# Expert layers of a decoder: blocks' results added to per-token sums in DRAM inside the loop, in place of a store by slot and a gather at the end

## What is computed

```python
logits = h @ gate_w.T                                  # h: [1024, 256]
scores = jax.nn.softmax(logits.astype(jnp.float32), axis=-1)
topk_w, topk_idx = jax.lax.top_k(scores, K)
cw = jnp.zeros((T, E), jnp.float32)
cw = cw.at[jnp.arange(T)[:, None], topk_idx].add(topk_w)
for e in range(E):
    g = h @ w_gate[e].T
    u = h @ w_up[e].T
    out = jax.nn.silu(g) * u @ w_down[e].T
    y = y + cw[:, e:e + 1].astype(x.dtype) * out
x = x + y
```

## Time and profile before

| | |
|---|---|
| three runs, us | 2011.71, 2017.87, 2011.18 (median 2011.71) |
| profiled execution, us | 2005.86 |
| its span, first to last instruction, us | 2004.0 |
| mean granted PE clock | 0.809 of full speed |
| PE busy | 1119.7 us (56%) |
| DVE busy | 1142.7 us (57%) |
| ACT busy | 473.7 us (24%) |
| POOL busy | 595.1 us (30%) |
| queue of SP's DMAs | 144.47 MB, 24.3% of 16 DMA engines |
| queue of POOL's DMAs | 31.26 MB, 5.9% |
| queue of ACT's DMAs | 19.93 MB, 3.1% |

### The profile page before, as it was taken

One profiled execution on the slowest core, in us unless ns is written; L12 is line 12 of the kernel. 1 busy time (PEld: TensorE's weight loads), 2 busy tenths in 40 slices (PEclk: granted clock), 3 DMA queues, 4 the chain that ended last, 5 costly groups with the idle time before them and its releaser, 6 DMA issues. The chain is left out here.

```text
span 2004.0 us, 21287 instructions
## 1 busy us (share of the span) xinstructions
PE 1119.7 (56%) x5620; PEld 707.5 (35%) x5620; DVE 1142.7 (57%) x1850; ACT 473.7 (24%) x881; POOL 595.1 (30%) x588
## 2 busy tenths in 40 slices
PE   5325536886054862552596704697566378537760
PEld 2202124664023640211354503575333034335540
DVE  5659974333354545998876694311357477463333
ACT  2143302221011444330211101332122266212220
POOL 0026614333620111661200081134302122043325
PEclk9659968998577886997798856899878599868985
DMA  6024335886307302331000011206500500357763
GB/s 203 2 85 147 104 106 167 261 263 188 94 8 147 45 2 87 130 121 63 0 0 1 0 16 27 85 1 181 174 8 2 170 21 3 121 160 213 220 191 102
DMA packets 146192, 196.51 MB, mean 98 GB/s; under 512 B 35056, under 2 KB 109954, under 8 KB 145484
## 3 DMA queue, kind: packets, MB, share of 16 engines
q1 hardware_dynamic: 109996, 144.47, 24.3%
q0 software_dynamic: 12608, 31.26, 5.9%
q10 hardware_dynamic: 23520, 19.93, 3.1%
HBM read 153.55 MB, written 41.75 MB: 97 GB/s over the span
## 5 line engine op out<-in xcount | busy, mean ns | idle before, releaser
L163 PE MATMUL psum<-w_ident,h 128*128 128x128 f32 x144 | 32.9, 423 | 188.3 <-DVE h L144 188.3
L453 PE MATMUL psum<-l0s_conv_out,w_ident 128*128 128x512 f32 x128 | 65.0, 632 | 83.4 <-DVE l0s_conv_out L550 83.4
L453 PE MATMUL psum<-l1s_conv_out,w_ident 128*128 128x512 f32 x128 | 65.6, 638 | 81.3 <-DVE l1s_conv_out L550 81.3
L1481 DVE TENSOR_REDUCE l3x_neg<-psum 128x2 f32<-128x512 f32 x128 | 80.9, 684 | 49.7 <-PE psum L1353 49.7
L163 PEld LDWEIGHTS psum<-w_ident,h 128*128 128x128 f32 x144 | 29.2, 224 | 191.7 <-DVE h L144 179.5
L175 ACT ACTIVATE hT<-psum 128x512 f32<-128x512 f32 x40 | 21.7, 595 | 310.4 <-PE psum L163 268.7
L933 PE MATMUL psum<-l0f_w_in,l0f_xT 128*128 128x352 f32 x224 | 79.1, 476 | 22.2 <-issue 12.4
L1456 ACT ACTIVATE l3x_work<-psum 128x512 f32<-128x512 f32 x128 | 72.5, 599 | 65.0 <-PE psum L1375 64.7
L152 POOL TENSOR_SCALAR rstd<-moments 128x8 f32<-128x8 f32 x12 | 2.9, 240 | 281.6 <-DVE moments L140 281.6
L933 PE MATMUL psum<-l3f_w_in,l3f_xT 128*128 128x192 f32 x256 | 64.5, 381 | 39.2 <-DMA l3f_w_in<-in_l3f_w_in 18.6
L419 POOL TENSOR_TENSOR l1s_xpad<-l1s_du,l1s_bc 128x1024 f32<-128x1024 f32 x32 | 75.2, 2352 | 32.5 <-DVE psum L546 32.4
(11 more groups left out here) (604 smaller groups left out, 3211.3 us busy)
## 6 DMA issues: line engine op xcount, KB each, us to landing
l0f_w_in<-in_l0f_w_in SPq DMA_DIRECT2D x56, 352.0 KB
l0s_bc<-l0s_scratch SPq DMA_DIRECT2D x16, 1024.0 KB, 5.1
l1s_bc<-l1s_scratch SPq DMA_DIRECT2D x16, 1024.0 KB, 5.2
l3f_w_in<-in_l3f_w_in SPq DMA_DIRECT2D x64, 192.0 KB
l0f_w_down<-in_l0f_w_down SPq DMA_DIRECT2D x56, 176.0 KB
l2f_w_in<-in_l2f_w_in SPq DMA_DIRECT2D x24, 352.0 KB
l3f_y_rows<-h SPq DMA_DIRECT2D x16, 512.0 KB, 6.8
l3f_y_rows<-l3f_y ACTq DMA_DIRECT2D x64, 128.0 KB
```

The source lines that it names most:

```text
L163: ins = nc.tensor.transpose(m.psum[:, at:at + P], m.h[:, t, k * P:(k + 1) * P], m.ident[:])
L453: ins = nc.tensor.matmul(m.pair(2 + c)[:, cols], lhsT=m.ident[:], rhs=rhs[:, cols], start=start, stop=stop, skip_group_check=True)
L1481: ins = nc.vector.tensor_reduce(self.neg[k % 2][:, :, hl], bank[:, 0:self.keys].rearrange("p (q k) -> p q k", q=self.maxima), AX_X, ALU.ma ...
```

## The change

The kernel keeps two arrays of per-token sums in DRAM, `sums[0]` and `sums[1]`, of 1024 rows and 128 more that take what unused slots give. SP sets them before the loop: zeros, or the residual in `sums[0]` where there is no shared expert. `h_rows` gets E more columns with the token's combine weights, so that a gather brings the weights along (`x` is [128, 256 + E]); where weights are divided by their sum, that is done earlier. In the gate multiplication DVE takes the weight as the scalar, in a column that it finds from the block's expert (a `value_load` per block). The `y` that leaves PSUM is thus weighted. POOL adds it to one of the two sums, even blocks to one and odd ones to the other, by an indirect transfer with `compute_op=ALU.add`, six blocks behind its gathers; an add waits until the add before it on the same side has landed. A gather now waits for `gate_done`, since `x` is needed until then. DVE's copy of `y` waits for `y_free`, which POOL raises with its adds. After the loop SP waits for all adds and loads both sums in four quarters into `m.h` and `m.hT`, and DVE adds them. The stores of `y`, the fills of `y_rows`, `slot_index`, `weight`, `back` and the final gathers are gone. The token table holds the token's number plus one, so that an unused slot is known by its zero.

```diff
-    x = ring("x", [P, D], GROUP)
+    x = ring("x", [P, D + E], GROUP)
...
-    h_rows = nc.dram_tensor(tag + "h_rows", (T, D), F32).ap()
-    y_rows = nc.dram_tensor(tag + "y_rows", (BLOCKS * P, D), F32).ap()
+    h_rows = nc.dram_tensor(tag + "h_rows", (T, D + E), F32).ap()
+    sums = [nc.dram_tensor(tag + f"sum{i}", (T + P, D), F32).ap() for i in range(2)]
+    landed = [m.h[:], m.hT[:].rearrange("p k (t d) -> p (k t) d", d=D)]
+    QUARTERS = 4
...
+    ADD_LAG = GROUP + 2
...
# SP
-            with sp.Fori(FEWEST, GROUPS) as i:
-                sp.dma_start(y_groups[bass.ds(i, 1)].rearrange("o b p d -> p (o b) d"),
-                             m.h[:, 0:GROUP, :]).then_inc(filled, 16)
+            sp.wait_ge(zeroed, 1)
+            for i in range(2):
+                start = m.resid[:] if i == 0 and not shared else zeros[:].unsqueeze(1).to_broadcast([P, TILES, D])
+                sp.dma_start(of_tiles(sums[i][0:T, :]), start).then_inc(sums_set, 16)
+                sp.dma_start(sums[i][T:, :], zeros[:]).then_inc(sums_set, 16)
+            sp.wait_ge(combined, 1)
+            sp.dma_start(of_tiles(h_rows[:, D:]), combine[:]).then_inc(h_stored, 16)
...
             by_steps(sp, groups, step, 0)
+            for i in range(2):
+                sp.wait_ge(added[i], groups * (16 * GROUP // 2))
+            per = TILES // QUARTERS
+            for q in range(QUARTERS):
+                for i in range(2):
+                    tiles = slice(q * per, (q + 1) * per)
+                    sp.dma_start(landed[i][:, tiles, :], of_tiles(sums[i][0:T, :])[:, tiles, :]).then_inc(sum_landed[q], 16)
# POOL
+            pool.sem_inc(y_free, GROUP)
-            pool.wait_ge(table_ready, 1)
-            pool.wait_ge(h_stored, 16)
+            pool.wait_ge(table_ready, 2)
+            pool.wait_ge(h_stored, 32)
+            pool.wait_ge(sums_set, 64)
...
                 if not first:
-                    pool.wait_ge(x_turned, base + (s - GROUP + 1))
+                    pool.wait_ge(gate_done, base + (s - GROUP + 1))
                     pool.sem_inc(may_gather, 1)
...
+            def add(base, s, early):
+                i, side = s - ADD_LAG, s % 2
+                if not early:
+                    pool.wait_ge(added[side], base * 8 + (i - 2 - side) * 8 + 16)
+                nc.gpsimd.tensor_copy(add_now[side][:], adds_to[:, bass.ds(base + i, 1)]).then_inc(add_token, 1)
+                pool.wait_ge(add_token, base + (i + 1))
+                pool.wait_ge(y_ready, base + (i + 2))
+                if not early:
+                    pool.sem_inc(y_free, 1)
+                else:
+                    pool.sem_inc(may_gather, 1)
+                nc.gpsimd.indirect_dma_start(
+                    sums[side], bass.IndirectOffsetOnAxis(ap=add_now[side][:, 0:1], axis=0), y[i % GROUP][:], None,
+                    compute_op=ALU.add).then_inc(added[side], 16)
             for s in range(GROUP):
-                pool.wait_ge(y_stored[s], groups * 16 + 16)
-            pool.sem_inc(may_gather, 1)
-            for q in range(K * TILES):
-                c, t = divmod(q, TILES)
-                if c:
-                    pool.wait_ge(accumulated, q - TILES + 1)
-                nc.gpsimd.indirect_dma_start(
-                    back[t][:], None, y_rows, bass.IndirectOffsetOnAxis(ap=slot_index[:, c, t:t + 1], axis=0)).then_inc(
-                        back_loaded[t], 16)
+                gather(0, s, True)
+            for s in range(GROUP):
+                gather(GROUP, s, False)
+                if s >= ADD_LAG - GROUP:
+                    add(GROUP, s, True)
+            with pool.Fori(2, groups) as i:
+                for s in range(GROUP):
+                    gather(i * GROUP, s, False)
+                    add(i * GROUP, s, False)
+            for s in range(ADD_LAG):
+                add(groups * GROUP, s, False)
# ACT
-                if not first:
-                    d = s - 4
-                    act.wait_ge(y_ready, base + (d + 2))
...
-                    act.dma_start(dst, y[d % GROUP][:]).then_inc(y_stored[d % GROUP], 16)
# DVE
-                    nc.vector.tensor_tensor(gated[d % 2][:], silu[d % 2][:], in_ps[d % 2][:, F:2 * F],
-                                            ALU.mult).then_inc(gate_done, 1)
+                    e = dve.value_load(owners[0:1, bass.ds(base + d, 1)], min_val=0, max_val=E - 1)
+                    nc.vector.scalar_tensor_tensor(out=gated[d % 2][:], in0=silu[d % 2][:],
+                                                   scalar=x[d % GROUP][:, bass.ds(e + D, 1)], in1=in_ps[d % 2][:, F:2 * F],
+                                                   op0=ALU.mult, op1=ALU.mult).then_inc(gate_done, 1)
...
-                    if not first:
-                        dve.wait_ge(y_stored[d % GROUP], base * (16 // GROUP) + (d // GROUP + 1) * 16)
+                    dve.wait_ge(y_free, base + (d + 1))
...
-            with dve.Fori(0, K) as c:
-                for t in range(TILES):
-                    dve.wait_ge(back_loaded[t], c * 16 + 16)
...
+            for q in range(QUARTERS):
+                tiles = slice(q * per, (q + 1) * per)
+                r = m.resid[:, tiles, :]
+                parts = [landed[i][:, tiles, :] for i in range(2)]
+                dve.wait_ge(sum_landed[q], 32)
+                if shared:
+                    o.link(dve, nc.vector.tensor_tensor(parts[0], parts[0], parts[1], ALU.add))
+                    o.mark(nc.vector.tensor_tensor(r, r, parts[0], ALU.add))
+                else:
+                    o.mark(nc.vector.tensor_tensor(r, parts[0], parts[1], ALU.add))
```

More of the change, by code:

```diff
@@ L652, in experts @@
     turns = sb(tag + "turns", [P, GROUPS])
-    slot, weight, block_of, lane_of = (sb(tag + s, [P, K, TILES]) for s in ("slot", "weight", "block_of", "lane_of"))
-    slot_index = sb(tag + "slot_index", [P, K, TILES], U32)
+    slot, block_of, lane_of = (sb(tag + s, [P, K, TILES]) for s in ("slot", "block_of", "lane_of"))
     owner, groups_f = sb(tag + "owner", [P, 1]), sb(tag + "groups_f", [P, 1])
@@ L675, in experts @@
     y = ring("y", [P, D], GROUP)
[L676 to L679 removed]
+    h_rows = nc.dram_tensor(tag + "h_rows", (T, D + E), F32).ap()
+    sums = [nc.dram_tensor(tag + f"sum{i}", (T + P, D), F32).ap() for i in range(2)]
+    of_tiles = lambda rows: rows.rearrange("(t p) d -> p t d", p=P)
+    landed = [m.h[:], m.hT[:].rearrange("p k (t d) -> p (k t) d", d=D)]
+    QUARTERS = 4
     bank = lambda i: m.psum[:, i * 512:(i + 1) * 512]
@@ L693, in experts @@
      lanes_ready, blocks_ready, tokens_ready, tabled, table_ready, h_stored, token_ready, x_turned, xT_ready,
-     in_done, silu_done, gate_done, g_turned, gT_ready, down_done, y_ready, filled, may_gather,
-     accumulated) = (
+     in_done, silu_done, gate_done, g_turned, gT_ready, down_done, y_ready, may_gather, combined, zeroed, sums_set,
+     add_token, y_free) = (
         sem(s) for s in ("logits", "less_max", "exps", "shared", "goes", "counted", "owner", "owners_filled",
                          "lists", "lanes", "blocks_of", "tokens", "tabled", "table", "h_stored", "token", "x_turned",
-                         "xT", "in_done", "silu", "gate", "g_turned", "gT", "down_done", "y", "filled",
-                         "may_gather", "accumulated"))
-    in_loaded, down_loaded, y_stored = (
-        [sem(f"{s}{i}") for i in range(GROUP)] for s in ("in_loaded", "down_loaded", "y_stored"))
-    x_loaded, back_loaded = m.gather_sems[tag]
+                         "xT", "in_done", "silu", "gate", "g_turned", "gT", "down_done", "y",
+                         "may_gather", "combined", "zeroed", "sums_set", "add_token", "y_free"))
+    in_loaded, down_loaded = ([sem(f"{s}{i}") for i in range(GROUP)] for s in ("in_loaded", "down_loaded"))
+    sum_landed = [sem(f"sum_landed{q}") for q in range(QUARTERS)]
+    x_loaded, added = m.gather_sems[tag]
     UNITS = shared * TILES
@@ L830, in _, with gather @@
                     number_tokens(pool, nc.gpsimd, c)
+            pool.sem_inc(y_free, GROUP)
             groups = group_count(pool)
-            pool.wait_ge(table_ready, 1)
-            pool.wait_ge(h_stored, 16)
-            def step(base, s, first, last):
+            pool.wait_ge(table_ready, 2)
+            pool.wait_ge(h_stored, 32)
+            pool.wait_ge(sums_set, 64)
+            def gather(base, s, first):
                 if s == 0:
@@ L965, in _ @@
                 shared_scalar(act)
-            for s in range(GROUP):
-                act.sem_inc(y_stored[s], 16)
             groups = group_count(act)
-            act.wait_ge(filled, (GROUPS - FEWEST) * 16)
             def step(base, s, first, last):
@@ L1085, in _ @@
             dve.wait_ge(tabled, K)
-            nc.vector.tensor_copy(token_of[:], table).then_inc(table_ready, 1)
-            o.link(dve, nc.vector.tensor_copy(slot_index[:], slot[:]))
-            if normalize:
```

(13 more changed lines are left out.)

39 lines of the change are left out of this document (25 added, 14 removed).

## The result

| | before | after |
|---|---|---|
| median of 4 executions, us | 2011.45 (1993.48 to 2017.87) | 2146.76 (2119.23 to 2156.54) |
| profiled execution, span, us | 2005.86, 2004.0 | 2149.08, 2147.2 |
| mean granted clock | 0.809 | 0.783 |

The ratio of after to before is 1.065 [1.059, 1.071]; it leaves out the 2156.54, an execution over 1.5% longer than the quickest of the same kernel. Forecast were 2069 us, 2.8% slower, in a range of 1990 to 2180: the sign and the range held, the size is more than double. On another chip, further down, the ratio was 1.051 [1.044, 1.059], some 103 us, 1.8 times the forecast's 57.

A forecast was written before the change was run, and what follows sets the result against it. PE and the weight stream set the old pace; POOL's issue work would become the bound. Loops +152.9, before the loops +1.7, tails -97.7 sum to +56.9 us on the 2011.7 median: 2069 us, 2.8% slower, range 1990 to 2180.

The forecast's parts named there:

- POOL becomes the bound: Expert loops: POOL's issue work sets 4.15, 3.80 and 3.94 us per block in l0f, l2f, l3f; +152.9 us; chance 54%.
- I take the gather's: Add issue on POOL in the loop: unseen in the trace, priced as a gather's, 0.95 us; upper bound twice that.
- add issues differ from 0.95: Sign that the forecast is wrong: an add's issue holds POOL for other than 0.95 us.
- that gap: POOL's loop: 0.30 us between a gather's issue and the copy of the add's indices, within 3.54 us per block.
- The group's rest: POOL, once per group of four: remaining wait for gathers' landing, 1.4 us in l0f, nothing in l2f, 0.56 in l3f.
- Hidden: Loop work said to fit under POOL's pace: DVE's register load (0.55 us), wider rows, gathers waiting for gate_done (some 3 us later).
- Tails of 33 us: After each loop's last gather: remaining adds, loads and DVE sums take about 33 us per stage, saving 97.7 us in all.
- The chain of adds: Rival, in loops and drains: one add at a time per side binds, at least (L + 1.29)/2 per block; 26%.
- the forecast's limits: Add landings above which the chain would bind at the forecast pace: 7.0, 6.3 and 6.6 us in l0f, l2f, l3f.
- The 2191 us: Time under the chain rival at landing L = 8, 4.65 us per block: 74 us more in loops, 36 and 12 in drains.
- More room for POOL: Rival: 0.47 instead of 0.86 us ahead of issues, no landing wait, 3.31 us per block; 1988 us, faster; 20%.
- the rule: Skill page's small descriptor generation: POOL free almost at once, adds vanish into the loop, 1923 us; the forecast held the trace disagrees.

The follow-up runs named there:

- wide: Kernel after with the constant 'number' given 128 bytes per partition in place of 32, so tiles regain their old alignment: 1.055 [1.052, 1.059] of before.

## Why the prediction was right in sign and too small

- **POOL becomes the bound: right.** Gather and add alternate, PE waits for x, POOL's busy share rises from 0.35 to 0.64 in l0f, and moving work off POOL gives 119.2 us of the loops back (`wide` beside the version with ACT's copies).
- **"I take the gather's": the step that failed.** Between bounds of 0.94 and twice that the add was put at 0.95; it took 1.60. The row nearest in form (same rows, same index) had no operation in it, and the operation is what costs. Without the operation the loops come out within 7.6 us of the forecast (500.5 for 508.1). The forecast itself named this sign of being wrong: "add issues differ from 0.95". Per block POOL takes 3.94 instead of 3.54: 0.65 more for the add, 0.05 for the gather, and 0.30 less, since the copy follows the gather with no gap. So a second term, that gap, was wrong the other way and hid nearly half of the first: 0.65 over 116 intervals would be 75 us.
- **Where the 50.0 us of the loops are.** 40.4 lie behind the eighth gathers and 9.6 ahead of them. Of the 116 intervals behind them, 87 take 3.94 to 4.02 us (medians) instead of 3.54, some 37 us together. In the other 29 a group ends, and POOL waits for a landing anyway, so that the add's price hardly shows: 3 us.
- **The group's rest.** Forecast 1.4, none and 0.56 us of landing per group; measured 13.4/12 = 1.1 in l0f, 5.8/4 = 1.5 in l2f and 9.2/15 = 0.6 in l3f. From the eighth gather on (331.85, 1400.86 and 1869.22) a block takes 4.39, 4.48 and 4.31 us in the mean, against 4.15, 3.80 and 3.94.
- **"Hidden": right only under this cover.** The wait for `gate_done` by itself costs 2.1% in the kernel before. In the kernel after it shows at the start, where the fifth to seventh gathers wait for the gate and no add is there yet: first to eighth gather take 17.8, 18.0 and 16.5 us, 9.6 more in sum than the forecast has. The register load on DVE by itself cost nothing (1.001 [0.997, 1.004]); beside the later release that wasn't shown.
- **Tails of 33 us: right in size**, 32.0, 33.2 and 31.5 (in l0f 18.1 to the last add for 18.2 forecast, 3.8 for 4.3, 10.1 for 10), but the 18.1 by luck. The forecast let the landing pace the last adds, at 2.65 us each. In l0f POOL's own work does it, 1.57 + 0.2 + 0.85 = 2.6 us; only one wait for a landing, of 0.27 us, stands among the last six adds. With the forecast's own price of 0.95 POOL's work would be 2.0 us per add, under the landing's 2.65. With plain scatters, at 1.00, the last six do come every 2.61 us, with waits for a landing or for `y` between them.
- **Not in the sum:** after the last sum DVE starts the next norm after 0.69 us where it had waited 7.37 in l0f for the stage change; such ends gave 9.6 us. No run took them apart.
- **Not foreseen: 44 us in stages that nothing touches.** Of the gap of 86.3 us between the difference of the two profiles and the forecast's this is half, and its cause is open; in three more profiles of the kernel after l3x, its largest part, took 258.2, 249.6 and 248.4.
- **The chain of adds: refuted.** Adds land in 4.9, 4.7 and 3.9 us in the median of l0f, l2f and l3f (4 was taken for an undisturbed one, and 3.7 is the quickest), under the forecast's limits of 7.0, 6.3 and 6.6. The 2191 us beside it was also said to be nearly what an add issue of twice a gather's gives; at 1.7 times, 2147 came. That 2147 lies in the range is luck in part: the chain set the upper end, and it did not bind.
- **More room for POOL: refuted**; the 0.84 to 0.88 ahead of an issue stayed in the loop. Nor did the rule hold that the forecast weighed, the Trainium skill's (DMA: Bandwidth & Descriptors, Anatomy of one DMA) "small" descriptor generation: 0.99 us for each gather and 1.60 for each add are 2.6 of the 3.94 us of a block. The forecast's "0.95 in each of the 140 gathers" is their median; the earlier trace rows have 0.94 to 1.30.

## What to carry to other kernels

Price an indirect transfer by what it holds GpSimd for, and one with an operation separately from one without: look for a row that has the operation, or keep its upper bound in the forecast. Where a transfer moves from the end into a loop, let an engine with room prepare its indices, so that GpSimd issues and does nothing else; that, with the wait for all gathers that went with it, decided between 5.5% slower (`wide`) and 1.6% faster. And a wait that is free because something else is late is not free: ask what it costs once the late one is mended.

## What the runs showed of the hardware

- An indirect store of 128 rows of 1 KB with an addition holds GpSimd for 1.60 us, the same store without it for 1.00, a gather of such rows for 0.95 in the kernel before and 0.99 in the kernel after. The next issue follows 0.30 later, but a copy follows at once.
- The addition takes 96 packets more for each 128 rows, for the same bytes: POOL's queue had 28,160 packets with it and 14,720 without, and held the 16 DMA engines for 236 instead of 131 us.
- The addition landed 3.7 us after the start of its issue at the quickest, 6.4 at the slowest beside the weight stream of l0f; a gather at the quickest after 2.8. Of the 0.9 between the quickest, 0.6 is as much as the issue is longer by.
- A copy that GpSimd makes for its own next issue costs 0.20 and 0.84 of waiting. With ACT making the copies, and no wait for all gathers, the three loops took 436.5 us instead of 555.7.
- The same 11,360 packets, stores to DRAM and loads back into SBUF, took 30.3 or 59.9 us of the 16 DMA engines in two programs that give them the same work.
